# A Mamba-style layer on one core: small products placed elsewhere in TensorE's slots, silu ahead of an evacuation, and the last states copied by ScalarE

## The reference, cut to what matters

```python
x  = gn(x) @ in_proj_w.T                     # 768 -> 1536 channels
xs = silu(depthwise_conv3x3(x) + conv_b)
dt, Bs, Cs = split(xs @ x_proj_w.T)          # 48 + 4 + 4 columns
delta = softplus(dt @ dt_w.T + dt_b)
dA    = exp(delta * A)                       # 4 states per channel
state[l] = dA[l] * state[l-1] + (delta * xs * Bs)[l]   # a scan over all 4096 pixels
y   = sum_n state * Cs + D * xs
out = layernorm(y) @ out_proj_w.T            # 1536 -> 768
x   = x + out
```

## Time and profile before

| | before |
|---|---|
| median of 3 runs | 3892.75 us (3892.51 to 3893.79) |
| profiled execution | 3894.47 us, of which the span from first to last instruction 3892.7 us |
| TensorE (PE) busy | 3479.1 us, 89% |
| VectorE (DVE) busy | 2988.7 us, 77% |
| ScalarE (ACT) busy | 2287.7 us, 59% |
| GpSimd (POOL) busy | 2345.4 us, 60% |
| mean granted TensorE clock | 0.943 of 2.4 GHz |

### The profile page before, as it was taken

How to read it: one execution, slowest core, us unless ns; L and a number is a source line. 1 busy time by engine, 2 the same in 40 slices (tenths; PEclk the granted TensorE clock), 3 DMA queues, 4 the chain that set the end, 5 groups by cost and what they waited for, 6 DMA issues and landing times. The chain is left out here.

```text
span 3892.7 us, 39046 instructions
## 1 busy us (share of the span) xinstructions
PE 3479.1 (89%) x10696; PEld 1744.0 (45%) x10696; DVE 2988.7 (77%) x4466; ACT 2287.7 (59%) x3710; POOL 2345.4 (60%) x1557
## 2 busy tenths in 40 slices
PE   4875799999999899999989999998797999999999
PEld 4422233333333344333333333333245877767787
DVE  4459999999999979999999999999853345555532
ACT  1356767777777757776777777776534555432211
POOL 0138888888888868887888888888840001112211
PEclk7887899999999999999999999998898999999999
DMA  7234445545545544555555455554633223355654
GB/s 272 85 133 106 103 127 136 152 126 141 133 131 149 145 118 120 141 134 132 146 142 140 126 139 142 137 144 100 176 97 109 65 71 103 107 172 200 198 194 154
DMA packets 217034, 529.85 MB, mean 136 GB/s; under 512 B 24728, under 2 KB 45784, under 8 KB 213872
## 3 DMA queue, kind: packets, MB, share of 16 engines
q1 hardware_dynamic: 173808, 376.32, 30.5%
q0 software_dynamic: 43008, 151.02, 17.6%
HBM read 346.11 MB, written 80.48 MB: 110 GB/s over the span
## 5 line engine op out<-in xcount | busy, mean ns | idle before, releaser
L578 PE MATMUL p_op<-uy,wout_ring 128*128 128x512 f32 x2160 | 1060.0, 640 | 134.1 <-DVE x_res L936 134.0
L562 PE MATMUL p_in<-xn,win_v 128*128 128x512 f32 (+1 forms) x2304 | 1056.3, 609 | 76.7 <-ACT halo L735 43.4
L897 DVE TENSOR_TENSOR_SCAN p_da<-p_da,state,g_ring 128x512 f32<-128x512 f32 x672 | 827.3, 1277 | 121.2 <-ACT p_da L698 98.5
L869 POOL TENSOR_TENSOR g_ring<-du,B_bc 128x2048 f32<-128x2048 f32 x192 | 870.1, 4532 | 17.0 <-DMA B_bc<-bc_scratch 2.1
L922 DVE SCALAR_TENSOR_TENSOR p_cv<-win_v,conv_w,p_cv 128x512 f32<-128x512 f32 x960 | 722.9, 753 | 105.2 <-ACT p_cv L756 84.2
L578 PEld LDWEIGHTS p_op<-uy,wout_ring 128*128 128x128 f32 x2160 | 421.0, 203 | 771.3 <-issue 591.4
L562 PEld LDWEIGHTS p_in<-xn,win_v 128*128 128x128 f32 x2304 | 445.6, 197 | 657.4 <-issue 657.4
L698 ACT ACTIVATE p_da<-delta,A 128x512 f32<-128x512 f32 x768 | 496.8, 678 | 323.2 <-DVE g_ring L907 322.0
L907 DVE TENSOR_TENSOR g_ring<-p_da,C_bc 128x512 f32<-128x512 f32 x768 | 494.9, 686 | 1.1 <-issue 1.1
L1356 PE MATMUL banks<-x_split,w_split 128*128 128x512 f32 x1152 | 464.0, 403 | 24.9 <-DVE w_split L1536 19.7
L1358 PE MATMUL banks<-x_split,w_split 128*128 128x512 f32 x1152 | 451.7, 392 | 0.0
(11 more groups left out here) (212 smaller groups left out, 4029.9 us busy)
## 6 DMA issues: line engine op xcount, KB each, us to landing
g_ring<-g_ring POOLq DMA_DIRECT2D x192, 512.0 KB, 5.2
win_v<-in_win SPq DMA_DIRECT2D x192, 384.0 KB, 3.2
wout_ring<-wout_scratch SPq DMA_DIRECT2D x184, 384.0 KB, 3.7
x_ring<-x_scratch SPq DMA_DIRECT2D x192, 256.0 KB, 2.7
q_scratch<-q_ring POOLq DMA_DIRECT2D x96, 256.0 KB, 2.4
x_split<-q_scratch SPq DMA_DIRECT2D x96, 256.0 KB, 3.2
out<-x_ring POOLq DMA_DIRECT2D x96, 256.0 KB, 2.8
x_res<-in_x SPq DMA_DIRECT2D x90, 256.0 KB, 4.2
```

Of the source, the lines that this page charges most:

```text
L562: last = nc.tensor.matmul(p_in[:, 0:n], WR[:, i % NW, t, :], XN[:, t, off:off + n], start=(t == 0), stop=(t == XT - 1))
L578: last = nc.tensor.matmul(p_op[:], OR[:, e % NO, k - h * HALF, :], ucol(c * K + k), start=(k == 0), stop=(k == K - 1))
L869: nc.gpsimd.tensor_tensor(G[:, i % NG], DU[:].unsqueeze(1).broadcast_to([P, NS, N]), BB[:], ALU.mult).then_inc(s_dbu, 1)
L897: nc.vector.tensor_tensor_scan(bank, bank, G[:, i % NG, n, :], init, ALU.mult, ALU.add)\
```

## The change

Five things are done in layer 0.

1. `keep_state` moves from VectorE to ScalarE. It now waits until both `times_c` are done, and `decay(i, 2)` and the next slot's `decay(.., 0)` wait for it.
2. On ScalarE the second copy of `x_dbl` (L783) goes ahead of `decay(i, 2)` and `decay(i, 3)` in slot 3.
3. In slots with S % 4 = 2 the Silu with its two table loads goes ahead of the evacuation.
4. The first group of x_proj products moves from slot 1 to slot 0. In slot 0 the whole half `out_proj` goes ahead of the norm sums.
5. In slot 3 (chunks with `within`) the first `delta_pair` goes into `in_proj`, after its fourth product, and the second one right behind `in_proj`, ahead of all six `out_proj` products.

```diff
-        S_XP, S_LN, S_OP = (13, 13, 14), 31, 31
+        S_XP, S_LN, S_OP = (12, 13, 14), 31, 31
...
-                def in_proj(i, fold_of):
+                def in_proj(i, fold_of, pair_of, S):
...
                         if t == 3 and fold_of is not None:
                             fold_xproj(fold_of)
+                        if t == 4 and pair_of is not None:
+                            delta_pair(pair_of, S)
...
+                    inside = within and to_fold is not None and group is not None
...
-                        in_proj(new, to_fold if within else None)
+                        in_proj(new, to_fold if within else None, NSP * group if inside else None, S)
                     if group is not None:
-                        delta_pair(NSP * group, S)
+                        delta_pair(NSP * group + (2 if inside else 0), S)
+                    c, m, h = half_at(S)
+                    if c is not None and S % K == 0:
+                        out_proj(c, m, range(h * HALF, (h + 1) * HALF))
...
                     c, m, h = half_at(S)
+                    if S % K == 0:
+                        c = None
                     if c is not None:
                         out_proj(c, m, range(h * HALF, h * HALF + 3))
-                    if group is not None:
+                    if group is not None and not inside:
                         delta_pair(NSP * group + 2, S)
...
+                def keep_state(i, p):
+                    act.wait_ge(s_cm, NS * i + 2 * p + 2)
+                    nc.scalar.activation(ST[:, i % K, 2 * p:2 * p + 2], p_da[:, :, N - 1], ACT.Copy).then_inc(s_scp, 1)
...
-                    if i is not None:
-                        decay(i, 2)
-                        decay(i, 3)
                     c = chunk_at(S, S_XP[2] + 1)
                     if c is not None:
                         act.wait_ge(s_xf, c + 1)
                         nc.scalar.activation(XD[:], p_dt[:, 1, :], ACT.Copy).then_inc(s_xd, 1)
+                    if i is not None:
+                        keep_state(i, 0)
+                        act.wait_ge(s_scp, 2 * i + 1)
+                        decay(i, 2)
+                        decay(i, 3)
...
-                    if new is not None and S % K and q is None:
+                    if new is not None and S % K and q is None and S % 4 != 2:
                         evacuate(new)
...
                         nc.scalar.activation(o, o, ACT.Silu).then_inc(s_silu, 1)
                         nc.scalar.preload_act_table_set(EXPSET)
+                    if new is not None and S % K and S % 4 == 2:
+                        evacuate(new)
...
+                    i = tile(S, L_SCAN)
+                    if i is not None:
+                        keep_state(i, 1)
                     i = tile(S, L_CH)
                     if i is not None:
+                        wait(act, s_scp, 2 * i)
                         decay(i, 0)
                         decay(i, 1)
...
-                def keep_state(i, p):
-                    vec.wait_ge(s_scan, NS * i + 2 * p + 2)
-                    nc.vector.tensor_copy(ST[:, i % K, 2 * p:2 * p + 2], p_da[:, :, N - 1]).then_inc(s_scp, 1)
...
-                        keep_state(a, 0)
...
-                        keep_state(a, 1)
```

More of the change, by code:

```diff
@@ L673, in _ @@
                             first_row(new)
-                        in_proj(new, None)
+                        in_proj(new, None, None, S)
                     if new is not None and not within and (S + 1) % K:
```

## The result

The changed kernel takes 3774.56 us (median of 4, 3772.5 to 3777.99) against 3892.63 (median of 4): a ratio of 0.9697, 95% interval 0.968 to 0.9714. It is 118 us faster; 103 had been forecast (3790 us, range 3758 to 3832).

The account below looks back on a forecast made before the run. Layer 0 was taken as bound by TensorE with ScalarE in slots 0 to 3, VectorE in 4 to 11. Savings of 74 (ordinary cycles), 11, 9, 7 and 1 us made 102, giving 3790 us, range 3758 to 3832.

Parts of the forecast that it names:

- What bounds it: Layer 0 cycles: TensorE's chain with ScalarE's sets slots 0 to 3, VectorE sets slots 4 to 11.
- keep_state off VectorE: Layer 0 half slots: 0.19 us saved per copy, 4.6 us per cycle; ScalarE's copy 0.2 us; 0.5 us stall in slot 6.
- Slot 0, and slots 1 to 3 on TensorE: The 3.13 us wait goes, 1.1 us idle at full speed; in_proj 0 at 8.3 us, fold at 43.9.
- Silu ahead of the evacuation: Slot 2: the 3.86 us stall before slot 3 goes; nothing is lost behind the evacuation in slots 6 and 10.
- Slot 3: New VectorE stalls of 1.9 us before scan 2 and 2.0 before slot 4; slots 0 to 3 take 53.5 us.
- The sum: A cycle of 157.0 us plus 0.8 for handoffs, 157.8; all terms together save 102 us.
- The two short ones: Two of the 13 cycles, 161.4 us with an input strip one row shorter: 2 x 5.5 = 11 us saved.
- the long one: The 187.0 us cycle, first chunk of the second image: 9 us saved.
- (A): New handoffs in slots 0 and 3 take back 2 to 4 us of 12 cycles: 3815 to 3840 us; chance 0.16.
- (B): ScalarE becomes the bound; slower from 1.0 us per copy, near 3940 us at 1.3; chance 0.03.
- (C): Slot 3's stalls close too: 154 us a cycle, 3745 to 3760 us; chance 0.08.
- (D): Only the copies count, TensorE's placement moves no end: 3850 us; chance 0.05.

Follow-up runs that it names:

- xd_behind_decays: The changed kernel with ScalarE's second copy of x_dbl in slot 3 back behind decays 2 and 3: 3764.86 us, ratio 0.9676 to the kernel before.
- x_dbl_behind: The changed kernel with both of ScalarE's copies of x_dbl in slot 3 behind the state copy and decays 2 and 3: 3766.82 us, ratio 0.9677.
- copies_twice: The changed kernel with each state copy made twice on ScalarE, once into a tile that nobody reads: 3772.46 us, ratio 0.9693.

## Why the prediction was right, point by point

**What bounds it.** VectorE in slots 4 to 11, TensorE with ScalarE in slots 0 to 3: shown. Moving the copies alone shortens slots 4 to 11 by 3.1 us and slots 0 to 3 by nothing; placing TensorE's products alone shortens slots 0 to 3 by 3.8 us and slots 4 to 11 by 0.4; and the Silu's stall moves from slot 3 to slot 4 when it is the only thing mended.

**keep_state off VectorE.** 0.19 us per copy forecast; 0.225 measured (an even slot fell from 12.04 to 11.59 us, two copies). In the timeline the product starts 0.21 us closer to its scans: it now starts 0.10 us before the pair of scans ends, where it had started 0.11 us behind the end. On ScalarE 170 ns, 0.2 forecast.

**Slot 0, and slots 1 to 3 on TensorE.** Every step within 0.2 us of the forecast, full clock after the wait for XN included.

**Silu ahead of the evacuation.** No stall before slot 3, and next to nothing lost behind the evacuation in slots 6 and 10: in the cycle looked at, `in_proj` waits 0.33 us for it in slot 7 and not at all in slot 11. What the prediction didn't see is that this is worth nothing in an ordinary cycle once TensorE's products are placed anew; it priced the parts together, so the sum isn't hurt. ScalarE's fuller slots cost what was said in kind: 0.37 us of stall in slot 6 (0.5 forecast), but also 0.6 us at the end of slot 11, for which room had been seen.

**Slot 3.** Both new stalls at their sizes. The prediction put down the first one, of 1.9 us, as a price and not as a fault; xd_behind_decays shows that putting x_dbl's copy ahead of the decays costs 0.9 us of each ordinary cycle in slot 3. So item 2 of the change, taken by itself, is a loss. One handoff came out right by some luck: the 1.06 us from the fold's start to the copy was read where ScalarE had only just finished its decays (1075.92 + 1.29 against a start at 1077.18), so it showed no more than an upper bound; it measured 1.06 again (1029.70 to 1030.76).

**The sum.** 102 us forecast, 119.3 between the profiled executions. Ordinary cycles 82 us for 74: the 0.8 us of handoffs put on the sum was not needed. That the bare steps gave 157.0 to the tenth is partly luck: in slots 4 to 11 of the cycle looked at VectorE's work came to 102.4 us (103.0 forecast) and its stalls to 1.1 (0.5 forecast), and the two misses cancel. The two short ones 15.8 for 11, the long one 5.9 for 9. Slots 17 to 35 give 1.2 for 7: there VectorE is 6.7 us less busy, but waits 10.3 us for decays where it waited 2.1. The last 16 slots with layer 1 took 1.3 us back, where 1 had been forecast as gain. These misses nearly cancel as well: the terms of the forecast, 102 us, measured 103.4 together.

The term that was missing is the start-up, 15.9 us, and it is nearly the whole distance between forecast and time. The result lies inside the range because the range was wide enough for it, not because the sum allowed for it. 8.35 us of it are won before `in_proj` of slot 12 starts (at 227.24 us before, 218.89 after). There ScalarE's evacuation of a first row had stood behind the Silu in slots 6 and 10, and `in_proj` of slots 7 and 11 waited 3.2 us each for it; all waits around the first twelve `in_proj` fell from 22.3 to 17.6 us. First the row of slot 11 before, then after:

```profile
210.33 7.08 PE L562 MATMUL p_in<-xn,win_v 128*128 128x512 f32 x12 [3.24 <-ACT win_v L710]
```

```profile
203.53 5.39 PE L564 MATMUL p_in<-xn,win_v 128*128 128x512 f32 x12 [0.49 <-ACT win_v L722]
```

The other 7.56 us come between there and the first scan, where TensorE had waited for the Silu of slot 14. First the row of the kernel before, then the same group after:

```profile
253.78 2.74 PE L667 MATMUL p_dt<-uy,xproj_w 128*64 128x512 f32 x8 [4.08 <-ACT uy L811]
```

```profile
240.74 1.94 PE L675 MATMUL p_dt<-uy,xproj_w 128*64 128x512 f32 x8
```

By the experiments the Silu's order makes most of it (13.5 us when taken back, 9.9 alone), the x_proj group some (3.7 and 7.8). Part is the clock's. The twelve `in_proj` of the first chunk are the same products behind nearly the same waits (17.6 to 18.4 us in all) in the changed kernel, xd_behind_decays, x_dbl_behind and copies_twice, but each takes either 5.39 us or 7 to 8, and together they take 76.6, 73.5, 81.5 and 82.9 us, at a mean granted clock of 0.87, 0.88, 0.84 and 0.83 in this stretch. From `in_proj` of slot 12 on, the four need 40.6 to 41.6 us to the first scan, and the kernel before needs 49.2. In the kernel before the twelve took 80.1 us, so some 3.5 of the 15.9 us can't be told from such chance, and some 12 are the change's.

**The rivals.** (A) would show as a gap over 2 us before `in_proj` 0 or inside it: 0.96 us and none. (B) is out at 170 ns a copy. The Trainium skill ("ScalarE: Activation LUTs", Rules for kernel authors) gives adds and multiplies to VectorE rather than ScalarE; it does not name copies. On the bare price the trace agrees (159 ns on VectorE, 170 on ScalarE), but the price did not decide: moving the copies to ScalarE alone made the kernel 41 us faster. (C) didn't come, as slot 3 has 4.15 us of stall. (D) has the size of what the copies alone gave (3852, for 3850), but the whole change wins nearly three times as much.

## What to carry to other kernels

Where engines take turns at being late, cut one period of the pipeline out of the timeline and add up the new order step by step between the starts of instructions: here that gave 157.0 us for a cycle of 157.0, with 0.6 us of misses that cancelled, while the shares of busy time said nothing. Compare such a sum with the parts of the cycle and not only with its total. Removing one stall in such a chain often moves it to the next handoff, so price the parts of a change together: in the ordinary cycles they added up to 116.5 us alone and gave 81.7 together. On an engine that works in order, put what is ready ahead of what still waits: the one part of this change that did the opposite, x_dbl's copy ahead of the decays, cost 0.9 us of an ordinary cycle. And do the same sum for the start-up, which this prediction left out.

## What the runs showed of the hardware

- A copy of two columns from two PSUM banks takes ScalarE 170 ns (384 of them), and a second one right behind the first starts 0.07 us later.
- Between scans and the product that follows, a 159 ns copy on VectorE costs 0.21 to 0.225 us, more than its own length. Without it the product starts 0.10 us before the scans end (994.80 against 994.90); with it the copy starts 0.03 us behind their end and the product 0.08 us behind the copy's start.
- The same products of TensorE in the 13 cycles were busy 1992.7 us before, 1954.1 after, and 1953.2 with the placing alone, which goes with the granted clock's rise from 0.96 to 0.98. Waits of 0.96 and 0.95 us in slots 0 and 1 were followed by products at full speed (5.39 us for 12 records). In the start-up, waits of 1.03 and 0.49 us around each `in_proj` went with either speed, 5.39 us or 7.08, and twelve of them took 73.5 to 82.9 us in four kernels that have the same code there.
